# Bodies of 40 steps in the main loops and of 32 in the loops at both ends, instead of 8

## What is computed

```python
def block(x, shift):                      # 6 heads of 8 channels, windows of 7 x 7 tokens
    h = layernorm(x)
    h = windows(roll(h, -shift))          # 64 windows of 49 tokens for each image
    q, k, v = split(h @ qkv_w + qkv_b)
    a = softmax(q * 8 ** -0.5 @ k.T + bias[rel_index] + mask)   # mask only where shift = 3
    x = x + roll(unwindow(a @ v @ proj_w + proj_b), shift)
    return x + gelu(layernorm(x) @ fc1_w + fc1_b) @ fc2_w + fc2_b
```

## Time and profile before

| | |
|---|---|
| median of 3 runs | 7914.44 us |
| profiled execution | 7950.78 us |
| its span | 7949.1 us |
| TensorE (matmul) busy | 7443.8 us, 94% |
| VectorE busy | 3710.7 us, 47% |
| ScalarE busy | 4083.7 us, 51% |
| GpSimd busy | 2232.5 us, 28% |
| mean granted clock of TensorE | 0.947 |

### The profile page before, as it was taken

The page is one execution under the profiler, slowest core; times in us unless marked ns, Lnnn a source line. Parts: engine busy times, 40 slices in busy tenths (PEclk is TensorE's granted clock), DMA queues, the critical chain, the costliest instruction groups (busy, mean ns, idle before and its releaser), DMA issues.

```text
span 7949.1 us, 332425 instructions
## 1 busy us (share of the span) xinstructions
PE 7443.8 (94%) x144058; PEld 5332.6 (67%) x144058; DVE 3710.7 (47%) x7474; ACT 4083.7 (51%) x6145; POOL 2232.5 (28%) x2070
## 2 busy tenths in 40 slices
PE   6879999999999999999999999999999999999997
PEld 4856666666666676666666666676666666666664
DVE  5154444444444444444444444444444444444443
ACT  0035555555555555555555555555555555555551
POOL 3023223223232332322222222233223223222320
PEclk9999999999999999999999999999999999999995
DMA  7000000000000000000000000000000000000007
GB/s 228 1 18 21 22 20 21 22 21 22 20 22 20 22 22 21 22 20 20 20 22 20 20 22 21 20 22 23 20 22 22 19 22 22 19 22 20 22 18 213
DMA packets 287397, 242.85 MB, mean 31 GB/s; under 512 B 42174, under 2 KB 281760, under 8 KB 285856
## 3 DMA queue, kind: packets, MB, share of 16 engines
q1 hardware_dynamic: 241506, 179.61, 8.4%
q10 hardware_dynamic: 36414, 19.95, 0.8%
q0 software_dynamic: 8192, 22.49, 0.8%
HBM read 112.73 MB, written 109.18 MB: 28 GB/s over the span
## 4 chain that ended last, share of the span: by engine, by line
PE 84%; DVE 8%; issue 5%; DMA 3%; ACT 0%; SPq 0%; POOL 0%; POOLq 0%; DVEq 0%; ACTq 0%
PE pA L969 15%; PE pS L927 11%; PE pS L940 7%; PE pA L890 6%; PE pB L1026 5%; DVE V L716 4%; PE pA L1018 4%; PE pB L1009 4%; PE pB L1047 4%; PE pS L949 4%; PE pB L1066 4%; PE pA L896 3%; PE pB L978 3%; PE pA L986 3%; PE pA L1057 2%
## 5 line engine op out<-in xcount | busy, mean ns | idle before, releaser
L438 POOL TENSOR_TENSOR Kbd<-KT,headmask 128x588 f32<-128x588 f32 x768 | 895.4, 1166 | 3735.3 <-DVE KT L702 3735.3
L691 DVE TENSOR_REDUCE mx<-pS 113x12 f32<-113x588 f32 x1536 | 1180.4, 769 | 1162.2 <-PE pS L949 1146.7
L927 PE MATMUL pS<-bias,stackr 128*128 128x296 f32 x6096 | 1385.7, 351 | 3.5 <-ACT E L498 3.3
L482 ACT ACTIVATE sq<-pB 112x392 f32<-112x392 f32 x768 | 379.4, 494 | 1949.9 <-PE pB L978 1949.9
L498 ACT ACTIVATE E<-pS 113x588 f32<-113x588 f32 x1536 | 1006.7, 655 | 650.6 <-DVE mx L691 622.1
L438 POOL TENSOR_TENSOR Qbd<-Qt,headmask 128x588 f32<-128x588 f32 x768 | 895.9, 1166 | 1479.8 <-DVE Qt L696 1479.8
L969 PEld LDWEIGHTS pA<-E,V 113*64 113x64 f32 x36864 | 1149.8, 142 | 115.1 <-issue 114.9
L927 PEld LDWEIGHTS pS<-bias,stackr 128*128 128x128 f32 x6096 | 973.2, 197 | 342.7 <-issue 206.2
L969 PE MATMUL pA<-E,V 113*64 113x49 f32 x36864 | 1198.8, 227 | 0.8 <-ACT va L487 0.8
L940 PE MATMUL pS<-Kbd,Qt 24*49 24x147 f32 x24576 | 784.3, 311 | 0.0
L949 PE MATMUL pS<-Qbd,KT 27*49 27x147 f32 x24576 | 724.3, 291 | 0.0
(11 more groups left out here) (126 smaller groups left out, 10061.5 us busy)
## 6 DMA issues: line engine op xcount, KB each, us to landing
xin<-xT SPq DMA_DIRECT2D x384, 98.0 KB, 2.0
xT<-xout SPq DMA_DIRECT2D x384, 98.0 KB, 1.9
xin<-xT SPq DMA_DIRECT2D x384, 73.5 KB, 1.9
xT<-xout SPq DMA_DIRECT2D x384, 73.5 KB, 1.8
xT<-cm POOLq DMA_DIRECT2D x128, 171.5 KB, 3.6
cm<-xT SPq DMA_DIRECT2D x128, 171.5 KB, 3.4
tm<-in_x SPq DMA_DIRECT2D x128, 147.0 KB
out<-tm ACTq DMA_DIRECT2D x128, 147.0 KB
```

What stands on the lines that cost most here:

```text
L438: return pool.tensor_tensor(y, x, m, ALU.mult)
L691: dve.tensor_reduce(m, s, AX.X, ALU.max).then_inc(mx_done, 1)
L927: mm(pS[:, q, S1:S1 + 2 * SW], stackr[:, :], rows, start=True, stop=False)
```

## The change

`UN`, the number of steps in a body, becomes 32 for the first and the last loop. A new constant `UM` = 40 takes its place in the sweep. As a step's number depends on the body's length, `Step` now carries it (`un`). The number of the first steps of `Fori(1, STEPS // UN)`'s loops that stand written out ahead of them goes from 8 to 32.

```diff
--- before.py
+++ after.py
@@ -28,7 +28,8 @@
 IMG = H * W
 TP, TK = 98, 4
 NPH = 3
-UN = 8
+UN = 32
+UM = 40
 XB = 8
 HP = HEADS // 2
 HC = HP * D
@@ -43,30 +44,30 @@
 class Step:
 
 
-    def __init__(self, u, c, t=0):
-        self.u, self.c, self.t = u, c, t
+    def __init__(self, u, c, t=0, un=UN):
+        self.u, self.c, self.t, self.un = u, c, t, un
 
     def val(self, scale, add):
 
-        return self.u * (UN * scale) + (self.c * scale + add)
+        return self.u * (self.un * scale) + (self.c * scale + add)
 
     def uses(self, of):
 
-        return self.u * (UN // of) + self.c // of
+        return self.u * (self.un // of) + self.c // of
 
     def last(self):
 
-        return isinstance(self.u, int) and self.t == NPH - 1 and UN * self.u + self.c == STEPS - 1
+        return isinstance(self.u, int) and self.t == NPH - 1 and self.un * self.u + self.c == STEPS - 1
 
     def next(self):
 
-        if isinstance(self.u, int) and UN * self.u + self.c == STEPS - 1:
-            return Step(0, 0, self.t + 1)
-        return Step(self.u, self.c + 1, self.t)
+        if isinstance(self.u, int) and self.un * self.u + self.c == STEPS - 1:
+            return Step(0, 0, self.t + 1, self.un)
+        return Step(self.u, self.c + 1, self.t, self.un)
 
     def before(self, n):
 
-        return isinstance(self.u, int) and self.t == 0 and UN * self.u + self.c < n
+        return isinstance(self.u, int) and self.t == 0 and self.un * self.u + self.c < n
 
     def mod(self, of):
         return self.c % of
@@ -288,19 +289,19 @@
 
             ahead = (1, 0, -1, -2, -3, -4)
             begin = 5
-            full = (STEPS - begin - 2) // UN
+            full = (STEPS - begin - 2) // UM
 
             def peeled(i):
-                iteration(*(Step(0, (i + k) % STEPS, (i + k) // STEPS) if 0 <= i + k < NPH * STEPS else None
+                iteration(*(Step(0, (i + k) % STEPS, (i + k) // STEPS, UM) if 0 <= i + k < NPH * STEPS else None
                             for k in ahead))
 
             for i in range(-1, begin):
                 peeled(i)
             for t in range(NPH):
                 with eng.Fori(0, full) as u:
-                    for k in range(UN):
-                        iteration(*(Step(u, begin + k + o, t) for o in ahead))
-                for i in range(begin + UN * full, STEPS + (begin if t < NPH - 1 else 4)):
+                    for k in range(UM):
+                        iteration(*(Step(u, begin + k + o, t, UM) for o in ahead))
+                for i in range(begin + UM * full, STEPS + (begin if t < NPH - 1 else 4)):
                     peeled(i + t * STEPS)
 
 
@@ -385,8 +386,8 @@
                 for part in range(2):
                     sp.dma_start(piece(j.t + 1, j, part), xout[:, b, mine(part)]).then_inc(out_st[b], 16)
 
-            load(Step(0, 0))
-            load(Step(0, 1))
+            load(Step(0, 0, 0, UM))
+            load(Step(0, 1, 0, UM))
 
             def iteration(a, b, c, d, e, f):
                 if a and not a.last() and not a.next().last():
```

## The result

| | before | change |
|---|---|---|
| median, us | 7908.74 (4 runs, 7892.82 to 7923.93) | 7554.93 (4 runs, 7546.86 to 7559.47) |
| profiled execution, us | 7950.78 | 7559.47 |
| its span, us | 7949.1 | 7557.8 |
| mean granted clock | 0.947 | 0.985 |

The ratio is 0.9552, 95% interval 0.953 to 0.9574. The prediction was 7552 us, 0.954 of before; the median fell by 353.8 us where 362 were forecast. The time of the profiled execution fell by 391.3 us.

The account below looks back on a forecast made before the run. The prediction took a chain of TensorE matmuls to bound the kernel, with time lost at loop back edges. From the median 7914.4 us it took 362 for 36 removed edges, other terms 0, giving 7552 us (0.954), range 7515 to 7620.

Parts of the forecast that it names:

- The search for the time: Sweep steps: 422.7 us lost at 42 loop back edges, as TensorE standing in "issue" and a lower clock behind it.
- Removed: 36 x 10.06 = 362 us: Sweep loops: 6 back edges instead of 42, each removed one saving the mean price of 10.06 us.
- 14 of the 56 waits before L1018: TensorE's unexplained idle, 161.5 us: 14 cases not edges, so an edge's share is at most 3.8 us.
- The end loops at 0: Rearrangements of x and output: transfers bound them, so longer bodies cost 0; at most 46 us gained in each if uncovered.
- Left: 6 x 10.06 = 60 us: Sweep's six remaining back edges: 60 us at the mean price, bounds 30 (all shortest) to 103 us (all longest).
- The other engines at 0: Sweep edges: other engines may stall 3.7 to 4.0 us each, covered by TensorE's stall; uncovered, up to 24 us more.
- Rival 1: Remaining sweep edges all long, other engines' stalls added: 7619 us at most; chance 0.07 for beyond 7600.
- The code read per step: Instruction queue: nearly everything run was also read, 62 bytes per instruction; longer bodies read the same number, cost zero.
- the sign of being right: First instruction queue: again near 1250 packets, less one for each edge.
- Rival 2, stalls within the bodies,: Sweep bodies: other engines wait for code mid-body, some 95 stalls, up to 8500 us; chance 0.03 past its threshold.
- The stretch without an edge: Sweep, 23 steps: ScalarE and VectorE pass 450 to 550 new instructions at 17.9 us a step, evidence against mid-body stalls.
- Rival 3, a clock that falls for want of pauses,: Sweep: like stops come back elsewhere, TensorE's clock lowered, half the gain gone, 7733 us; chance 0.06, shared with partial mid-body stalls.

Follow-up runs that it names:

- e3: The change, but sweep bodies of 40 steps on TensorE alone and 8 on the four other engines: 7556.7 us, ratio 0.9565 to before.
- e4: The change, but sweep bodies of 8 steps on TensorE and 40 on the four other engines: 7779.7 us, ratio 0.986 to before.
- e5: The change with one sweep body of 120 steps on every engine, no back edge left in the sweep: 7490.8 us, ratio 0.9492 to before.
- e6: The change with one sweep body of 120 steps on TensorE and bodies of 8 on the four others: 7507.0 us, ratio 0.9519 to before.
- e1: The kernel before with only the first and last loop at 32 steps a body, sweep left at 8: 7788.4 us, ratio 0.9894.
- e2: The kernel before with only the sweep at 40 steps a body, end loops left at 8: 7562.9 us, ratio 0.9567.

## Why the prediction was right, and where only its sum was

*The search for the time* held: the loss was at the back edges, TensorE's own, and nowhere else. e3 and e4 separate the engines, and e5 and e6 remove the last edges.

*Removed: 36 x 10.06 = 362 us.* The total is right to 8 us (353.8 measured). As a price of an edge the 10.06 is not: it is the price where the loops of the kernel before happened to lie, in the slowest of its executions on record. Carried to the median it is about 9.1, by which 36 edges are 326 us and not 362; and the six that are left cost 27.5 us and not 60. The two errors have opposite signs, and that the sum is right to 8 us is luck in part. The profiled execution, for which 7589 us were written down, came to 7559.5. In e1 the same 42 edges cost 6.05 each.

The prediction says that 14 of the 56 waits before L1018 are not edges. The trace of before has all 56 at the 42 edges: in the third phase TensorE stands there twice. The 3.8 us are thus no upper bound but the mean of these waits, and with the 0.7 us before L1026, which the prediction left out, 4.6 us of the 10.06 are idle time.

The 354 us can also be read in two steps: 104 us from the new `UN` alone, by its moving of TensorE's code, and the other 230 to 250 us (7788.4 or 7806.3 to 7554.9) from the 36 edges, 6.5 to 7 us each. The two don't add: the change of `UM` alone (e2) has 7562.9, since few edges are left for the place to act on.

*The end loops at 0* was right for the loops, 2.7 us more and 2.0 less, and wrong for the edit: I looked at what the edit does in its loops, and not at what it moves behind them. In the full change this cost nothing, for the reason just given. With `UM` left at 8, as in e1, it would have made the forecast wrong by 100 us.

*Left: 6 x 10.06 = 60 us.* Measured 27.5 us, 4.6 each (5.2 against the change's own steps), near the shortest (5.0) of the kernel before and inside the bounds of 30 to 103 us only by the second way of counting. TensorE stands 3.7 us at an edge instead of 4.6, and none of the six is long; one in e3 and two in e2 are, so this too is partly chance.

*The other engines at 0.* Right, and for the reason given: VectorE and GpSimd now do stand at an edge, 2.9 and 1.9 us, beneath TensorE's 2.87. The rule of "Runtime: NRT & Kernel Launch" in the Trainium skill, section "Instruction fetch mechanics", that a taken branch out of a small instruction store waits for a fetch, agrees: the second queue went from 31 to 291 packets, and the stalls appeared. Rival 1, which used it, overstated what it would cost. The price of a branch in "Advanced Engine Details and Errata" of the Trainium skill, section "Control Flow Timing", about 108 ns, is not what an edge of this loop costs: 4.6 us on average even in the change.

*The code read per step.* The remark that nearly all that ran was also read holds for TensorE alone. That didn't enter the sum. The first instruction queue carried 1168 packets where the sign of being right was 1250 less one for each edge: 86 fewer for 36 edges in the sweep and 24 in the end loops. The end loops alone took 11 off (e1).

*Rival 2, stalls within the bodies,* fell. The four engines read nine times the packets, and no step in mid-body is longer than before. Its packets of 16.4 KB are TensorE's; those of the second queue are of 8.2 KB (2.38 MB in 291), so there were twice as many places for such a stall as it counted. The stretch without an edge that it sets against them passes fewer new instructions than the 450 to 550 it names: 129 + 194 = 323 on ScalarE and some 340 on VectorE, by the table of the change. *Rival 3, a clock that falls for want of pauses,* fell too: 717.9 us without an edge at 17.95 us a step, and a mean clock of 0.985 where 0.98 was forecast. e5 and e6 have no edge in some 6700 us, and a mean clock of 0.988.

*The profiled execution fell by 391 us, the median by 354.* The profiled execution of before was 42 us above its median, that of the change 5. If it is partly chance whether an edge is short or long, a kernel with 42 of them should scatter more, and it does: 7870 to 7951 us over all its runs here, against 13 us between the lowest and highest of the change. The clocks on record go with it: 0.959 in the execution of 7870 us, 0.951 in that of 7938, 0.947 in the profiled one. That this one had more long edges than most is likely by that, but no trace of another execution shows it.

## What to carry to other kernels

Where a loop's body runs long on the engine that bounds the kernel, measure the distance between two equal instructions across the back edge and within the body; here the difference was 10 us for each return, half of it idle time marked "issue" and half the lower clock behind it, and no group of instructions showed either. Lengthen the body on that engine first, and to a single run if the program's size allows it. And don't take a price measured at one place in the code, in one execution, as a constant: code that is put ahead of a loop moves it, and the fastest and the slowest execution of one kernel differ by 1% (7870 and 7951 us).

## What was not expected of the hardware

- The place of TensorE's code changes what a back edge costs: about 9.1 us in the kernel before, 6.3 to 6.5 in three kernels at two other sets of places (estimates, carried to the medians). Whether TensorE stops once or twice goes with where the loop's head lies in its piece of 256 instructions: once at six places from 43 to 126, twice at five from 171 to 238. Why the clock stays low for long at some edges was not settled.
- A stop of TensorE of 9.6 or 20.4 us costs itself and 2.4 or 2.2 us of slower matmuls; at the edges of before and of the kernels with other places, of 3.5 to 4.6 us idle, it is 2.2 to 5.5. In 3 to 17 cases of 42 the lower clock lasts for some 30 us and costs about 9 more. After a stop of 2.27 us it didn't fall at all (e1's first edge).
- The other engines find a loop of 8 steps (90 to 221 instructions on GpSimd, ScalarE and VectorE) without reading it again, and don't find one of 40 (410 to 1069): 37 against 291 packets of 8.2 KB. They stood for it, VectorE 2.9 and GpSimd 1.9 us at the edge shown, but it cost no time here, as TensorE stood as long (7556.7 and 7554.9 us).
- In a kernel whose loops run once, a step was 0.06 to 0.10 us shorter. The loop's register arithmetic goes with it; that this is the reason was not isolated.
